# Three attention stages in one kernel: another DVE order in the cross stage, a triangle mask from 32-partition matmuls, another piece table in the second stage

## The reference, cut to what matters

```python
B, S, C, H = 16, 256, 128, 16          # batches, tokens, channels, heads
x = x + tanh(g_xattn[0]) * L0_xattn(layernorm(x), ctx)   # stage a: causal self attention, D = 8, plus attention to ctx (64 tokens)
x = x + tanh(g_ffn[0])   * L0_ffn(layernorm(x))          # stage c
# L1_xattn:
u = LN(xx); u = u + mha(u, u, causal)                    # stages d (attention) and e (its MLP), D = 32
u = LN(u);  u + mha(u, ctx, not causal)                  # stages f (attention) and g (its MLP), D = 32, 64 keys
x = x + tanh(g_ffn[1]) * top1_experts(layernorm(x))      # sort, tiles, gather

# one attention, per batch and head
s = q @ k.T * D ** -0.5
s = where(row >= column, s, -inf)                        # stage a: the mask before the softmax
a = softmax(s);  o = a @ v                               # stage d: the mask after it; stage f: none
out = (o of all heads side by side) @ wo + bias
```

## Time and profile before

| | us |
|---|---|
| median of 3 runs | 1652.21 (1650.4 to 1652.48) |
| the profiled execution | 1654.29 |
| its span, first to last instruction | 1652.5 |
| mean granted TensorE clock | 0.922 |

### The profile page before, as it was taken

How to read it: one execution, slowest core, us unless ns; L and a number is a source line. 1 busy time by engine, 2 the same in 40 slices (tenths; PEclk the granted TensorE clock), 3 DMA queues, 4 the chain that set the end, 5 groups by cost and what they waited for, 6 DMA issues and landing times. The chain is left out here.

```text
span 1652.5 us, 56201 instructions
## 1 busy us (share of the span) xinstructions
PE 1350.0 (82%) x22797; PEld 855.1 (52%) x22798; DVE 935.6 (57%) x2365; ACT 708.6 (43%) x1493; POOL 737.4 (45%) x1263
## 2 busy tenths in 40 slices
PE   4899999999977959999999986969888969705860
PEld 2555555555545725555555554645554537605860
DVE  3466666666634656777777754456566556611431
ACT  1455555555534426556656652414333324302430
POOL 3233333333322837787787774842222125351016
PEclk9999999999997979999999997979989879856995
DMA  4340000000000310000000001210101013201114
GB/s 103 104 128 16 20 16 19 17 19 13 13 12 26 96 51 12 22 22 12 22 22 19 9 12 58 79 48 21 29 26 29 21 56 111 63 37 47 55 59 135
DMA packets 129455, 69.42 MB, mean 42 GB/s; under 512 B 20312, under 2 KB 125356, under 8 KB 129212
## 3 DMA queue, kind: packets, MB, share of 16 engines
q1 hardware_dynamic: 127164, 61.75, 13.3%
q0 software_dynamic: 2048, 4.20, 0.8%
HBM read 41.80 MB, written 24.12 MB: 40 GB/s over the span
## 5 line engine op out<-in xcount | busy, mean ns | idle before, releaser
L595 ACT ACTIVATE space<-scores 128x512 f32<-128x512 f32 x576 | 314.1, 551 | 344.8 <-PE scores L454 258.2
L681 DVE TENSOR_REDUCE space<-scores 128x2 f32<-128x512 f32 (+1 forms) x512 | 308.7, 624 | 223.2 <-PE scores L454 150.9
L823 POOL TENSOR_SCALAR_AFFINE_SELECT space<-space 128x512 f32<-128x512 f32 x128 | 81.6, 637 | 290.0 <-ACT space L595 290.0
L425 PE MATMUL scores<-space 32*128 32x256 f32 (+1 forms) x2304 | 196.8, 411 | 16.3 <-DVE space L681 10.5
L835 POOL TENSOR_TENSOR space<-space 128x1024 f32<-128x1024 f32 x64 | 151.5, 2368 | 0.0
L454 PE MATMUL scores<-space 32*128 32x256 f32 (+1 forms) x2048 | 149.7, 357 | 0.0
L425 PEld LDWEIGHTS scores<-space 32*128 32x128 f32 x2304 | 94.7, 188 | 99.8 <-DVE space L681 75.5
L827 POOL TENSOR_SCALAR_AFFINE_SELECT space<-space 128x512 f32<-128x512 f32 x128 | 87.9, 687 | 71.6 <-ACT space L595 71.5
L401 PE MATMUL misc<-w_a_li_w,space 128*32 128x128 f32 x2048 | 74.7, 290 | 34.1 <-ACT space L1113 15.1
L454 PEld LDWEIGHTS scores<-space 32*128 32x128 f32 x2048 | 84.0, 187 | 16.7
L1084 ACT ACTIVATE space<-scores 128x512 f32<-128x512 f32 x64 | 37.9, 597 | 113.7 <-PE scores L994 90.0
(11 more groups left out here) (309 smaller groups left out, 2855.5 us busy)
## 6 DMA issues: line engine op xcount, KB each, us to landing
space<-in_x SPq DMA_DIRECT2D x32, 128.0 KB, 2.2
x<-space SPq DMA_DIRECT2D x16, 256.0 KB, 2.9
space<-xx SPq DMA_DIRECT2D x32, 128.0 KB, 2.1
xo<-space SPq DMA_DIRECT2D x32, 128.0 KB
space<-xo SPq DMA_DIRECT2D x16, 256.0 KB
space<-xm SPq DMA_DIRECT2D x32, 128.0 KB, 2.2
space<-x SPq DMA_DIRECT2D x16, 256.0 KB, 3.7
sorted_in<-zeros SPq DMA_DIRECT2D x10, 256.0 KB
```

What stands on the lines that cost most here:

```text
L425: last = pe.matmul(a.score_bank(j)[:, 0:n], q[rows, e * P:(e + 1) * P], keys[rows, 0:n], start=not cut, stop=True, skip_group_check=True)
L595: act.activation(pt[:, 2 * pair:2 * pair + 2, lo:S], a.score_banks(pair)[:, :, S + lo:2 * S], ACT.Exp, bias=0.0, scale=1.0)\
L681: last = dve.tensor_reduce(out[:, c % 2, 2 * pair:2 * pair + 2], banks[:, :, 0:n], AX.X, ALU.max, negate=True)
L823: pool.affine_select(out=block, in_=block, compare_op=ALU.is_ge, fill=0.0, base=0, pattern=[[0, 4], [1, P]], channel_multiplier=-1).then_i ...
```

## The change

Stage a: the triangle is written by matmuls that use 32 rows and all 128 columns of the array, as the scores after them do. `ident_parts[:, part]` holds, on each strip of 32 partitions, the 32x32 identity in columns 32 part to 32 part + 31. `above_parts[:, part]` holds the rows of `above` that belong to that part. So four matmuls, over 128, 96, 64 and 32 columns, add up to the block in each bank. The number of matmuls stays at 16 per unit. The two constants take 5 more fills on POOL and 12 more small instructions on DVE ahead of stage a.

Stage d: the transpose T moves from slot 5, bank 1, to slot 4, bank 0, and N of slot 5 from bank 0 to bank 1.

Stage f: DVE's order is now one table that also holds the saving of denominators (E), `norm_stats` (A) and `norm` (W). R and M of the first half move from the even slot to the odd one, `norm_stats` from the odd slot to the even one (and POOL's `rstd` with it), and Y of the even slot goes from bank 0 to bank 1 and to the end of DVE's slot. Each unit's denominators are transposed straight out of PSUM into a tile of their own, so that the copy, the sum and the transpose of the sum make place for two transposes.

```diff
--- before.py
+++ after.py
@@ -244,7 +244,7 @@
         1: [[(U, 0, -2)], [(N, 1, -1, 1), (R, 0, -2)], [(M, 0, -2), (V, 0, 0, 0)], [(T, 0, 1, 1)], [], [(N, 0, 0, 1)], [(Q, 0, 1, 0)],
             [(K, 0, 1, 1)], [(Y, 0, -2, 0)], []],
         4: [[(U, 0, -2), (Q, 1, 0, 0)], [(R, 0, -2), (N, 1, -1, 1), (V, 0, 0, 0)], [(M, 0, -2), (Q, 2, 0, 1)], [(R, 1, -2), (V, 1, 0, 0)],
-            [(M, 1, -2), (Q, 3, 0, 1)], [(N, 0, 0, 0), (T, 0, 1, 1), (Y, 0, -2, 0)], [(Q, 0, 1, 1)], [(Y, 1, -2, 0)]],
+            [(M, 1, -2), (Q, 3, 0, 1), (T, 0, 1, 0)], [(N, 0, 0, 1), (Y, 0, -2, 0)], [(Q, 0, 1, 1)], [(Y, 1, -2, 0)]],
     }
 
     def __init__(self, k, name, D, mask, src, base, dst, ctx, w):
@@ -418,8 +418,11 @@
         n, cut = S, a.mask == "before" and c < a.CROSS
         if cut:
             n = (e + 1) * P
-            for j in range(4):
-                strips(pe, a.score_bank(j)[:, e * P:n], k.identb[:, :], k.above[:, :], True, False)
+            for part in range(4):
+                for j in range(4):
+                    rows = slice(32 * j, 32 * j + 32)
+                    pe.matmul(a.score_bank(j)[:, e * P + 32 * part:n], k.ident_parts[rows, part], k.above_parts[rows, part, 32 * part:P],
+                              start=(part == 0), stop=False, skip_group_check=True)
         for j in range(4):
             rows = slice(32 * j, 32 * j + 32)
             last = pe.matmul(a.score_bank(j)[:, 0:n], q[rows, e * P:(e + 1) * P], keys[rows, 0:n],
@@ -857,12 +860,13 @@
 
     T, Q, K, V, N, Y = "TQKVNY"
 
-    U, R, M = "URM"
+    E, U, R, M, A, W = "EURMAW"
 
     LAG, PER = 3, 2
 
-    SLOTS = [[(N, 0, -1, 1), (Q, 0, 1, 0), (Q, 1, 1, 1), (K, 0, 1, 0), (U, 0, -3), (R, 0, -3), (M, 0, -3), (Y, 0, -4, 0)],
-             [(V, 0, 0, 0), (T, 0, 2, 1), (R, 1, -3), (M, 1, -3), (Y, 1, -4, 0)]]
+    SLOTS = [[(N, 0, -1, 1), (E, 0, 0, None), (U, 0, -3, None), (Q, 0, 1, 0), (Q, 1, 1, 1), (K, 0, 1, 0), (A, 0, 3, None), (W, 0, 2, None),
+              (Y, 0, -4, 1)],
+             [(E, 1, 0, None), (R, 0, -3, None), (V, 0, 0, 0), (T, 0, 2, 1), (M, 0, -3, None), (R, 1, -3, None), (M, 1, -3, None), (Y, 1, -4, 0)]]
 
     def __init__(self, k, name, src, base, dst, ctx, w):
         self.k, self.name, self.D, self.G = k, name, 32, QUADS
...
@@ -879,12 +883,7 @@
     def pieces(self, i):
 
         b, v = divmod(i, 2)
-        return [(p[0], p[1], b + p[2], p[3]) for p in self.SLOTS[v] if len(p) == 4 and 0 <= b + p[2] < B]
-
-    def steps(self, i):
-
-        b, v = divmod(i, 2)
-        return [(p[0], p[1], b + p[2]) for p in self.SLOTS[v] if len(p) == 3 and 0 <= b + p[2] < B]
+        return [(kind, n, b + d, bank) for kind, n, d, bank in self.SLOTS[v] if kind == self.E or 0 <= b + d < B]
 
     def is_unit(self, n):
         return 0 <= n < 2 * B
@@ -1015,7 +1014,7 @@
         wait(pe, s["den_saved"], n)
         pt = k.pt[:, n % TURNED]
         for j in range(4):
-            pe.matmul(k.num[32 * j:32 * j + 32, S:2 * S], k.ones_cross[:, u], pt[:, j, :], start=True, stop=True, skip_group_check=True)
+            pe.matmul(k.num[32 * j:32 * j + 32, S:2 * S], k.ones_cross[:, 0], pt[:, j, :], start=True, stop=True, skip_group_check=True)
         for j in range(4):
             for half in range(2):
                 rows, at = slice(64 * half, 64 * half + 64), (4 * (2 * u + half) + j) * 32
...
@@ -1143,27 +1143,28 @@
 
         b, u = divmod(n, 2)
         wait(dve, s["pv_done"], n + 1)
-        wait(dve, s["turned_den"], b - 1)
-        part = k.num[:, S:2 * S]
-        if u == 0:
-            last = dve.tensor_copy(k.dens[:, b % 2], part)
-        else:
-            last = dve.tensor_tensor(k.dens[:, b % 2], part, k.dens[:, b % 2], ALU.add)
-        last.then_inc(s["den_saved"].sem, 1)
+        wait(dve, s["rden"], b - 1)
+        dve.transpose(k.dens[:, b % 2, u], k.num[:, S:2 * S]).then_inc(s["den_saved"].sem, 1)
 
     def step(kind, n, b):
 
+        if kind == a.E:
+            if a.is_unit(2 * b + n - a.LAG - 1):
+                save_denominators(2 * b + n - a.LAG - 1)
+        if kind == a.A and b > 1:
+            norm_stats(Step(b))
+        if kind == a.W and b > 1:
+            norm(Step(b))
         if kind == a.U:
             wait(dve, s["den_saved"], 2 * (b + 1))
-            wait(dve, s["rden"], b)
-            dve.transpose(k.den[:, 0:S], k.dens[:, b % 2]).then_inc(s["turned_den"].sem, 1)
-            wait(dve, s["turned_den"], b + 1)
             wait(dve, s["r_full"], 2 * b)
-            dve.reciprocal(k.rsum[:, 0], k.den[:, 0:S].rearrange("p (q x) -> p q x", x=32)[:, :, 0:QUADS]).then_inc(s["rden"].sem, 1)
+            dve.reciprocal(k.rsum.rearrange("p n q c -> p (n q c)")[:, 0:32].rearrange("p (u q h) -> p u q h", u=2, q=8),
+                           k.dens[:, b % 2].rearrange("p u (q x) -> p u q x", x=32)[:, :, :, 0:2]).then_inc(s["rden"].sem, 1)
         if kind == a.R:
             wait(dve, s["rden"], b + 1)
             wait(dve, s["ot"], 2 * (b - 1) + n + 1)
-            spread = k.rsum[:, 0, :, 2 * n:2 * n + 2].rearrange("p q c -> p c q").unsqueeze(3).to_broadcast([P, 2, 8, 32])
+            turned = k.rsum.rearrange("p n q c -> p (n q c)")[:, 16 * n:16 * n + 16].rearrange("p (q h) -> p h q", h=2)
+            spread = turned.unsqueeze(3).to_broadcast([P, 2, 8, 32])
             dve.transpose(k.rx[:, n], spread).then_inc(s["r_full"].sem, 1)
         if kind == a.M:
             wait(dve, s["r_full"], 2 * b + n + 1)
@@ -1198,16 +1199,11 @@
     for i in a.slots:
         if a.is_unit(i):
             maxima(i)
-        if a.is_unit(i - a.LAG - 1):
-            save_denominators(i - a.LAG - 1)
         for kind, n, b, which in a.pieces(i):
-            piece(kind, n, b, which)
-        for kind, n, b in a.steps(i):
-            step(kind, n, b)
-        if i % 2 == 1 and 2 <= i // 2 + 3 < B:
-            norm_stats(Step(i // 2 + 3))
-        if i % 2 == 0 and 2 <= i // 2 + 2 < B:
-            norm(Step(i // 2 + 2))
+            if which is None:
+                step(kind, n, b)
+            else:
+                piece(kind, n, b, which)
 
 
 def gpsimd_cross(pool, a):
@@ -1242,7 +1238,7 @@
     for i in a.slots:
         if i % 2 == 1 and 0 <= i // 2 < B:
             split(i // 2)
-        if i % 2 == 1 and 2 <= i // 2 + 3 < B:
+        if i % 2 == 0 and 2 <= i // 2 + 3 < B:
             rstd(Step(i // 2 + 3))
         if i % 2 == 1 and 0 <= i // 2 - 3 < B:
             bias(i // 2 - 3)
@@ -2022,6 +2018,8 @@
         self.own8 = self.sb("own8", [P, 16])
         self.own_of_four = self.sb("own_of_four", [P, 4])
         self.own_thirds = self.sb("own_thirds", [P, 6, 4])
+        self.ident_parts, self.above_parts = self.sb("ident_parts", [P, 4, P], BF16), self.sb("above_parts", [P, 4, P], BF16)
+        self.eye, self.own_part, self.edge, self.own_above = (self.sb(n, [P, c]) for n, c in (("eye", 32), ("own_part", 4), ("edge", 32), ("own_above", P)))
         self.of_six = self.sb("of_six", [P, 6])
         self.selectors = self.sb("selectors", [P, 6, P], BF16)
         self.ones_column = self.sb("ones_column", [P, 4, 32])
...
@@ -2235,13 +2233,26 @@
 
     pe.transpose(k.num[:, 0:8], w.first_rows[:, :], k.ident[0:8, 0:8]).then_inc(r.filled, 1)
 
-    pe.wait_ge(r.result, 5)
+    pe.wait_ge(r.result, 9)
     pe.matmul(k.misc[:, 0:P], k.bv_b, w.raw_wp[:, :], start=True, stop=False)
     pe.matmul(k.misc[:, 0:P], k.bcv_b, w.raw_wp[:, :], start=False, stop=True).then_inc(r.filled, 1)
 
 
 def vector_first(dve, k, w, r):
     result = Count(r.result)
+    quarters = lambda x: x.rearrange("p (j x) -> p j x", x=32)
+    result.inc(dve.tensor_reduce(k.eye[:, :], k.ident[:, :].rearrange("p (j x) -> p x j", x=32), AX.X, ALU.add))
+    result.inc(dve.tensor_reduce(k.own_part[:, :], quarters(k.ident[:, :]), AX.X, ALU.add))
+    dve.wait_ge(r.result, result.n)
+    for part in range(4):
+        dve.tensor_copy(k.ident_parts[:, part, 32 * part:32 * part + 32], k.eye[:, :])
+    result.inc(dve.tensor_tensor(quarters(k.own_above[:, :]), quarters(k.above[:, :]),
+                                 k.own_part[:, :].unsqueeze(2).to_broadcast([P, 4, 32]), ALU.mult))
+    dve.wait_ge(r.result, result.n)
+    result.inc(dve.tensor_reduce(k.edge[:, :], k.own_above[:, :].rearrange("p (j x) -> p x j", x=32), AX.X, ALU.add))
+    dve.wait_ge(r.result, result.n)
+    for part in range(4):
+        dve.tensor_copy(k.above_parts[:, part, 32 * part:32 * part + 32], k.edge[:, :])
     result.inc(dve.tensor_reduce(k.of_six[:, :], k.own_thirds[:, :, :], AX.X, ALU.add))
     dve.wait_ge(r.result, result.n)
     dve.tensor_copy(k.selectors[:, :, :], k.of_six[:, :].unsqueeze(2).to_broadcast([P, 6, P]))
@@ -2420,6 +2431,11 @@
         keep(k.ones_cross[part], [[-2, 2], [1, 32]], -half, 0, ALU.not_equal, 1.0)
     pool.wait_ge(made.sem, made.n)
     fill(k.nmax3[:, :, :, :], 0.0)
+    fill(k.ident_parts[:, :, :], 0.0)
+    fill(k.above_parts[:, :, :], 0.0)
+    for part in range(3):
+        pool.wait_ge(made.sem, made.n)
```

(6 more changed lines are left out.)

6 lines of the change are left out of this document (3 added, 3 removed).

## The result

| | before | after |
|---|---|---|
| median, us | 1651.31 (4 runs, 1650.07 to 1652.48) | 1606.49 (4 runs, 1598.24 to 1615.47) |
| ratio to before | | 0.973, 95% interval 0.967 to 0.979 |
| profiled execution, us | 1654.29 | 1598.24 |
| its span, us | 1652.5 | 1596.5 |
| mean granted clock | 0.922 | 0.929 |

The forecast was 1601 us, for a profiled execution of 1603.8. The span is 56.0 us shorter. From the starts of the scores' matmuls in both traces (first window to last window of each stage) the difference splits as follows: stage a begins 1.7 us later (28.1 against 26.4), takes 424.7 us for 443.1 (-18.4), stage d 372.4 for 372.0 (+0.4), stage f 182.4 for 218.1 (-35.7). What lies between and behind the stages is 4.0 us shorter, spread over three stretches (-1.7, -0.7 and -1.6) in which the change touches at most the run-out of a stage. The sum of the forecast was +2 - 19 + 2 - 35.5.

The account below looks back on a forecast made before the run. It took TensorE's window in series with DVE's reductions to bound stages a and d, and waits behind ACT and DVE to slow stage f. 2 - 19 + 2 - 35.5 = -50.5 us from 1654.3 gave 1603.8 profiled, 1601 predicted, range 1591 to 1618.

Parts of the forecast that it names:

- Set-up, +2: Ahead of stage a: DVE's 12 more instructions cost 1.5 to 2.3 us, all on the path, taken as +2.
- Stage a, -19: Mask in stage a: 0.20 us off each window, passed on in six of eight causal slots, over 16 batches: -19 us.
- Rival (2): Stage a: mask rounds run one behind the other, the mask takes 0.5 to 0.6 us, total 1640; chance 0.06.
- Stage d, +2: Stage d: Y's 0.27 us wait goes, but DVE handles T first and delays slot 5's maxima: +2 us, bounds -4 and +8.
- a hole of TensorE: Stage d, slot 4: T fits between the last projections, streamed by 705.3, and the next window at 705.53.
- Rival (4): Stage d loses 0.5 us a batch, total 1608; chance 0.1.
- Stage f, -35.5: Stage f: ten batches go from 160.8 to 128 us (-33), the last two with scores give -2.5; ends -20 and -38.
- rival (1): Stage f: DVE becomes the bound, odd slot 6.4 us or more, batch 13.8 to 14 us, total 1616; chance 0.14.
- 0.4 us of DVE time of no account: Stage f: two transposes replace a copy, a sum and one transpose, saving DVE about 0.4 us per batch.
- The list of waits that go: Stage f: the 0.46 us wait for ACT's copy of K goes; that for V's copy falls from 1.29 to 0.2.
- Rival (3): Clock dips in stages a and d, 2.7 us each; one in each of 32 batches gives 1687; chance 0.03.
- the distance from profiled run to median (2.1 us): Whole kernel: the median lies 2.1 us below the profiled execution, so 1603.8 becomes 1601.7.

Follow-up runs that it names:

- the mask alone: The kernel before with only stage a's triangle from 32-partition matmuls and its two constants: 1635.43 us, ratio to before 0.990.
- the six later ones: Six runs of the changed kernel, unaltered, once more on another chip: median 1597.00 us, ratio to before 0.968.
- statistics moved: The changed kernel, but in stage d DVE does norm_stats in slot 3 instead of 4, and M before T in slot 4: 1597.01 us, ratio to before 0.966.

## Why the prediction was right, point by point

- **Set-up, +2.** Twelve instructions in 2.1 us, stage a starts 1.2 to 2.0 us later in the traces. Right.
- **Stage a, -19.** Measured -18.4 (-19.0 with the mask alone). Both halves of the step held: 0.20 us off the window, by a load that hides beside the last mask round, and six slots of eight that pass it on, the six that were named. The argument that carried it was a neighbouring pair of rows with the same tile shape, the one place where the trace of before showed what the new order of instructions would do. Rival (2), rounds one behind the other, is out: by it the load would have come 0.5 to 0.6 us after the start of the mask, not 0.14. Sixteen loads, four on each group of 32 rows, have begun within those 0.14 us, though one takes 0.09.
The Trainium skill, TensorE: Matmul & The Clock Gate, Part 3, says in its list of what overlaps that a weight load overlaps running matmuls only where the row group differs. This trace doesn't agree, at 0.14 us for four rounds on the same groups. The same part also lets a load go ahead into a background weight buffer, which would allow it; no run here shows which buffer a load went to.
- **Stage d, +2.** Measured +0.4. The mechanism is right (DVE handles T before M and the statistics, so the maxima wait in its queue; moving the two gives 0.47 us a batch back), but two terms were off. T was said to lie in a hole of TensorE; slot 4 grew by 0.24 us: in the earlier trace rows the next window began 0.67 us after the last projections, now T begins 0.54 us after them (688.28) and the window 0.37 behind T, so only 0.13 us of that time was a hole. And the maxima of slot 5 start 2.30 us after their window, not 2.7: T is ready sooner (688.76, 0.11 us after the window's start, not 0.32) and M is shorter, 0.68 for 0.82. The errors cancel, so that a full batch loses 0.02 us instead of 0.15, and that is luck. The first two batches lose 0.6 us each (19.66 to 20.30, 22.46 to 23.06), as forecast. Rival (4), half a microsecond a batch, is out.
- **Stage f, -35.5.** Measured -35.7; the batch 12.71 for 12.8, the ten batches -32.9 for -33. Waits: none in the even slot, about 0.13 us in the odd one, where 0 and 0.2 were said. DVE's odd slot: ends at 1174.52 with the next maxima at 1174.46, so full, as worked out, and rival (1) was near: a few tenths more in that slot and it would have been true. What was wrong inside the sum is the share of its parts. The denominators were booked as 0.4 us of DVE time of no account. They lie on the chain from Y's residual to the odd maxima and give 0.45 us a batch, and they are enough by themselves to end the dips. The order, which the text made the main thing, gives 1.28, but 0.58 of it is the wait for the copied maxima in the even slot. The list of waits that go leaves that one out, though the batch of 12.8 us counts it as gone.
- **The clock.** Full clock over the ten batches, as forecast (1.00). Rival (3) would have shown below 0.97 in stage a; it is 0.98. The reason given, that TensorE waits for under 3% of a batch, isn't needed for it: with waits of 0.83, 0.46 and 0.36 us in 14.52 the clock is as full.
- **From the profile to the median.** The profiled execution is 5.6 us below its forecast (1598.24 for 1603.8), 4.0 of them between and behind the stages, which the forecast left as they were. The median of four runs lies 5.5 above 1601, that of the six later ones 4.0 below. The range held both. So the stages bear the sum out to within 2 us, and how near the median came to 1601 is chance. I had taken the distance from profiled run to median (2.1 us) as if it were fixed; the runs show it as chance, from -10.6 (statistics moved) to +8.3 (after).

## What to carry to other kernels

Try small matmuls ahead of others in the shape of those: here one tile shape for the whole window took 0.15 us off a 0.34 us mask, and over a third fewer columns only 0.04. To price a step that stands in a queue, follow the chain without idle time that it is part of: 0.43 us taken out of such a chain gave 0.45 a batch, while a wait of 0.27 us, taken away where the engine behind was full, came back as 0.41 at the next window. And before a table is moved for one engine, list what the other engine must do first in that slot.

## What the runs showed of the hardware

- The clock of stage f fell to 1.2 GHz for 6.8 us at a time in every kernel with a wait of 1.29 us in each batch, and in none whose longest wait there was 0.84 us or less, though one of these is busy for only 128.54 of 145.73 us.
- After 13 us in which TensorE stood idle ahead of stage f, the granted clock stayed at half for 13.7 to 23.9 us, in two profiles with a second stretch of 20.5 us close behind; the stage took 192.4 and 197.8 us then. With 50 matmuls in that hole it was 3.4 us in one profile, with another 3.4 us ten us later, and none in the other.
- Four rounds of bf16 mask matmuls with 512 columns instead of 320 in all cost 0.04 us (0.184 against 0.142 from the first load to the scores' load), where 192 columns at 2.4 GHz would be 0.08. The scores' load starts within 0.01 us of the start of the last round, in both kernels, so the last round's columns (128 or 32) don't delay it. The first three rounds differ by 96 columns, which at 2.4 GHz is the 0.04.
- With 32x128 tiles on both sides, the f32 load starts 0.001 to 0.002 us after a bf16 matmul on the same 32 rows has started; where 128x32 tiles came first, it started 0.16 us after the start of their last round.
